# Attention with a routed feed-forward: row sums out of the bank ring, normalisations on ScalarE, expert order, one power on GpSimd

## What is computed

```python
router_probs = softmax(flat @ router_w + router_b)          # 8 experts
topk_probs, topk_idx = top_k(router_probs, 2)               # the other weights are 0
shared_out = gelu(flat @ sw1 + sb1) @ sw2 + sb2
h1 = gelu(einsum('td,edh->teh', flat, rw1) + rb1)           # hidden 256
mixed = einsum('ted,te->td', einsum('teh,ehd->ted', h1, rw2) + rb2, weights)
out = shared_out + mixed
```

## Time and profile before

| | |
|---|---|
| runs | 468.04, 468.20, 470.07 us; median 468.2 |
| the profiled execution | 470.0 us; its span, first to last instruction, 468.2 us |
| mean granted clock of TensorE | 0.984 of full speed |
| TensorE busy | 450.0 us (96%) |
| GpSimd, VectorE, ScalarE busy | 307.6, 276.1, 203.8 us |
| attention alone, then experts beside the end of attention | to about 395 us, then to 468 us |

### The profile page before, as it was taken

The page is one execution under the profiler, slowest core; times in us unless marked ns, Lnnn a source line. Parts: engine busy times, 40 slices in busy tenths (PEclk is TensorE's granted clock), DMA queues, the critical chain, the costliest instruction groups (busy, mean ns, idle before and its releaser), DMA issues.

```text
span 468.2 us, 7198 instructions
## 1 busy us (share of the span) xinstructions
PE 450.0 (96%) x2567; PEld 336.3 (72%) x2567; DVE 276.1 (59%) x517; ACT 203.8 (44%) x293; POOL 307.6 (66%) x203
## 2 busy tenths in 40 slices
PE   9999899999999999999999999999999999997995
PEld 7777566877676777776777777767776676775884
DVE  4687965957644669665246687642464157743443
ACT  3553231323354334333642343335334465784772
POOL 5959583667366586774665867654559894765773
PEclk9999897999999999999999999999999999998999
DMA  8300200000002000000030000000000000000000
GB/s 241 92 1 1 53 2 0 2 1 0 2 0 54 1 0 1 0 1 2 0 97 6 1 0 2 1 0 1 1 1 2 0 1 0 1 0 1 24 3 22
DMA packets 5194, 7.27 MB, mean 16 GB/s; under 512 B 644, under 2 KB 4136, under 8 KB 5160
## 3 DMA queue, kind: packets, MB, share of 16 engines
q1 hardware_dynamic: 5160, 6.81, 5.2%
HBM read 6.29 MB, written 0.52 MB: 15 GB/s over the span
## 4 chain that ended last, share of the span: by engine, by line
PE 82%; POOL 6%; DVE 5%; issue 5%; ACT 1%; POOLq 0%; ACTq 0%; DVEq 0%
PE ps L1094 20%; PE ps L1000 11%; PE ps L1077 10%; PE ps L1078 10%; PE ps L1079 10%; POOL g_lo L633 5%; PE ps L924 5%; PE ps L926 4%; PE ps L925 4%; PE ps L1012 2%; DVE ps L829 2%; PE ps L1018 1%; PE ps L1006 1%; PE ps L932 1%; DVE xn L771 1%
## 5 line engine op out<-in xcount | busy, mean ns | idle before, releaser
L697 ACT ACTIVATE probs<-ps 128x1024 f32<-128x1024 f32 (+1 forms) x112 | 107.8, 963 | 160.0 <-PE ps L1079 158.8
L486 POOL TENSOR_TENSOR work<-work,probs 128x1024 f32<-128x1024 f32 x60 | 142.7, 2378 | 44.9 <-ACT probs L697 42.7
L816 DVE TENSOR_REDUCE maxes<-ps 128x1 f32<-128x402 f32 x256 | 134.2, 568 | 31.9 <-PE ps L1000 31.3
L1094 PE MATMUL ps<-probs,v_sb 128*64 128x256 f32 (+1 forms) x832 | 98.1, 386 | 0.0
L1077 PE MATMUL ps<-g_hi,ctxT_hi 97*128 97x512 f32 (+1 forms) x208 | 84.2, 405 | 1.1 <-DVE g_hi L824 1.1
L1094 PEld LDWEIGHTS ps<-probs,v_sb 128*64 128x64 f32 (+1 forms) x832 | 57.4, 138 | 36.7 <-issue 9.8
L1000 PE MATMUL ps<-ctxT_hi,g_hi 96*128 96x402 f32 x256 | 79.8, 374 | 4.0 <-DVE maxes L816 2.0
L1078 PE MATMUL ps<-g_lo,ctxT_hi 96*128 96x512 f32 (+1 forms) x208 | 82.8, 398 | 0.0
L1079 PE MATMUL ps<-g_hi,ctxT_lo 96*128 96x512 f32 (+1 forms) x208 | 82.4, 396 | 0.0
L1000 PEld LDWEIGHTS ps<-ctxT_hi,g_hi 96*128 96x128 f32 x256 | 47.2, 191 | 23.9 <-issue 6.4
L829 DVE RECIPROCAL ps<-ps 128x256 f32<-128x256 f32 x16 | 28.3, 1766 | 57.3 <-PE ps L1012 57.3
(11 more groups left out here) (138 smaller groups left out, 572.8 us busy)
## 6 DMA issues: line engine op xcount, KB each, us to landing
raw<-in_ctx_T_dram SPq DMA_DIRECT2D x3, 600.4 KB, 4.4
work<-in_L_ffn_rw_dram SPq DMA_DIRECT2D x1, 1024.0 KB, 7.6
raw<-in_ctx_T_dram SPq DMA_DIRECT2D x3, 150.8 KB, 2.6
x_sb<-in_x_dram SPq DMA_DIRECT2D x1, 384.0 KB, 5.2
early<-in_WqkT_dram SPq DMA_DIRECT2D x1, 336.0 KB, 4.7
wo_sb<-in_L_xattn_Wo_dram SPq DMA_DIRECT2D x1, 256.0 KB, 5.6
out_dram<-x_sb SPq DMA_DIRECT2D x1, 256.0 KB, 2.2
out_dram<-x_sb SPq DMA_DIRECT2D x2, 128.0 KB, 1.7
```

Source lines behind the costliest of these rows:

```text
L486: ops.tensor_tensor(acc, acc, pr, ALU.add).then_inc(summed, 1)
L697: nc.scalar.activation(probs[0:rows, n % SLOTS, 0:wide, :], s, ACT.Exp, scale=SCALE).then_inc(probs_ready, 1)
L816: v.tensor_reduce(maxes[:, p % 2, i * T + t, blk:blk + 1], src[:, 0:BW], AX.X, ALU.max).then_inc(ring_taken, 1)
L1094: ins = mm(o_bank[DH * i:DH * (i + 1), :], v_sb[0:rows, c, h * DH:(h + 1) * DH], probs[0:rows, n % SLOTS, j, i * S:(i + 1) * S], start=(c ...
```

## The change

The row sums leave the ring for the first 14 pairs: they go into the bank that the one-chunk unit of the next pair leaves free, with semaphores of their own, and the score tile that next uses that bank waits until they are taken. The second layernorm step (`normal`, `norm`) is done by ScalarE as `rstd * x + shift`, except for the first batch's first one; GpSimd makes `shift`. The planner no longer counts `normal` and `norm` among VectorE's costs. `g` of the second pair is placed ahead of the last two `v0`. In the second half the shared expert comes last, and `wrow` goes before the first `spread`. VectorE makes the low parts of the last four items. The largest logit is subtracted on VectorE, so that the exponentials are one instruction; in the second half they are a power of e on GpSimd, and `best` is done by VectorE.

```diff
-DVE_US = {"max": 0.51, "g": 1.45, "shift": 0.72, "sums": 2.3, "y": 0.5, "yt": 1.8, "norm": 1.6, "xt": 0.95,
-          "xn": 1.5, "router": 0.5, "rank": 2.6, "wrow": 0.7, "stats": 1.3, "normal": 1.6}
+DVE_US = {"max": 0.51, "g": 1.45, "shift": 0.72, "sums": 2.3, "y": 0.5, "yt": 1.8, "xt": 0.95,
+          "xn": 1.5, "router": 0.5, "rank": 2.6, "wrow": 0.7, "stats": 1.3}
...
-            tasks += rest[:2] + [("shift", b, p)] + rest[2:] + [("g",) + order[1]]
+            tasks += rest[:2] + [("shift", b, p)] + rest[2:-2] + [("g",) + order[1]] + rest[-2:]
...
-                        main.append(("ring", ("sums", qb, qp)))
+                        main.append(("ring", ("sums", qb, qp)) if (b, p) == order[-1] else ("sums", (qb, qp)))
...
+        if name == "sums" and x[0] != "ring":
+            pe += PE_US[name]
+            dve = max(dve, pe + HOP_US) + DVE_US[name]
+            return
...
+def expert_order(half, experts):
+
+    return [experts] + list(range(experts)) if half == 0 else list(range(experts)) + [experts]
...
+            if h == 1 and turn == 0:
+                out.append(("ring", ("wrow", last)))
             if e < experts:
                 out.append(("ring", ("spread", h, e)))
...
-            if h == 1 and turn == 0:
-                out.append(("ring", ("wrow", last)))
...
+        def sums_bank(pair):
+
+            return s_bank((pair + 2) * NU - 1, 1)[:, 0:S]
...
+        LAST_SUMS = B * PAIRS - 2
+
+        def sums_done(pair):
+
+            w = ("sums",) + divmod(pair, PAIRS)
+            return (sums_taken, pair + 1) if pair < LAST_SUMS else taken(w)
...
-        LAST_LO = NI - HK
+        LAST_LO = NI - 2 * HK
...
-                    engine.wait_ge(ring_filled, ring_no[("sums",) + divmod(pair - 2, PAIRS)] + 1)
+                    engine.wait_ge(sums_filled, pair - 1)
...
             def inverse_roots(tiles, round_no):
                 pool.wait_ge(var_ready, round_no)
...
+                then_own(g.tensor_tensor(rstd[:, tiles], veps[:, tiles], neg_half[:, tiles], ALU.pow))
+                g.tensor_tensor(shift[:, tiles], neg_mean[:, tiles], rstd[:, tiles], ALU.mult).then_inc(rstd_ready, 1)
...
+            g.memset(euler[:], math.e)
...
+                if kind == "exp" and w == NHALF - 1:
+                    pool.wait_ge(logit_ready, w + 1)
+                    g.tensor_tensor(lexp[:], euler[:], logit[:], ALU.pow).then_inc(lexp_ready, 1)
+                if kind == "best" and w < NHALF - 1:
...
+            def normal(src, tiles, round_no):
+
+                act.wait_ge(rstd_ready, round_no)
+                for t in tiles:
+                    ins = nc.scalar.activation(xn[:, t, :], src[:, t, :], ACT.Identity, bias=shift[:, t:t + 1],
+                                               scale=rstd[:, t:t + 1])
+                ins.then_inc(xn_ready, 1)
...
+                elif kind == "normal":
+                    normal(x_sb, range(w * T, w * T + T), w + 1)
+                elif kind == "norm":
+                    if w == 0:
+                        act.wait_ge(*taken(("xn", 1)))
+                    normal(x1, range(w * T, (w + 1) * T), B + w + 1)
...
-                elif kind == "exp":
+                elif kind == "exp" and w < NHALF - 1:
                     act.wait_ge(logit_ready, w + 1)
-                    for t in range(TH):
-                        ins = nc.scalar.activation(lexp[:, t, :], logit[:, t, :], ACT.Exp,
-                                                   bias=neg_lmax[:, t:t + 1])
-                    ins.then_inc(lexp_ready, 1)
+                    nc.scalar.activation(lexp[:], logit[:], ACT.Exp).then_inc(lexp_ready, 1)
...
+                v.tensor_scalar(neg_mean[:, ts], mv[:, ts, 0], -1.0, None, ALU.mult)
...
+            def quotient(b, p, rden, signal):
+
+                pair = b * PAIRS + p
+                v.reciprocal(rden, rden).then_inc(rden_ready, 1)
+                dve.wait_ge(rden_ready, pair + 1)
+                dve.wait_ge(o_raw_ready, pair + 1)
+                v.tensor_tensor(oT[:, b % 2, p, :], o_raw[:], rden, ALU.mult).then_inc(signal, 1)
...
+                if kind == "sums":
+                    dve.wait_ge(sums_filled, w[0] * PAIRS + w[1] + 1)
+                    quotient(*w, sums_bank(w[0] * PAIRS + w[1]), sums_taken)
...
-                        v.tensor_reduce(neg_lmax[:], logit[:], AX.X, ALU.max, negate=True).then_inc(logit_ready, 1)
+                        then_own(v.tensor_reduce(neg_lmax[:], logit[:], AX.X, ALU.max, negate=True))
+                        v.tensor_tensor(logit[:], logit[:], neg_lmax[:].unsqueeze(2).to_broadcast([P, TH, E]), ALU.add
+                                        ).then_inc(logit_ready, 1)
...
-                elif kind == "norm":
-                    normal(x1, range(w * T, (w + 1) * T), B + w + 1)
...
+                elif kind == "best" and w == NHALF - 1:
+                    dve.wait_ge(ranked, w + 1)
+                    dve.wait_ge(wrow_zero, 2)
+                    then_own(v.tensor_tensor(weight[:], rprob[:, :, 0:E], low[:, :, 0:E], ALU.subtract))
+                    then_own(v.tensor_copy(w_hi[:], weight[:]))
+                    hi = w_hi[:].bitcast(F32)
+                    wr = wrow[:, w * TH:(w + 1) * TH, :]
+                    v.tensor_copy(wr[:, :, 0:E], hi)
+                    v.tensor_tensor(wr[:, :, WLO:WLO + E], weight[:], hi, ALU.subtract).then_inc(w_ready, 1)
...
+                if kind == "sums":
+                    pair = w[0] * PAIRS + w[1]
+
+                    pe.wait_ge(probs_ready, (pair + 2) * NU - 2)
+                    row_sums(*w, sums_bank(pair)).then_inc(sums_filled, 1)
...
+                    if u == 1 and j == 1 and n > 2 * NU:
+
+                        pe.wait_ge(sums_taken, min(b * PAIRS + p - 1, LAST_SUMS))
```

More of the change, by code:

```diff
@@ L16 @@
+import math
 from contextlib import ExitStack
@@ L211, in plan_experts @@
     for h in range(halves):
-        for turn, e in enumerate([experts] + list(range(experts))):
+        for turn, e in enumerate(expert_order(h, experts)):
             new = list(range(n, n + chunks))
             out += [("first", i) for i in new]
+            if h == 1 and turn == 0:
+                out.append(("ring", ("wrow", last)))
             if e < experts:
@@ L298, in build @@
         rstd = sb("rstd", [P, NT])
+        shift = sb("shift", [P, NT])
+        neg_mean = sb("neg_mean", [P, NT])
         neg_half = sb("neg_half", [P, NT])
@@ L349, in build @@
         lexp = sb("lexp", [P, TH, E])
+        euler = sb("euler", [P, TH, E])
         lsum = sb("lsum", [P, TH])
@@ L455, in build @@
         block = ctx.enter_context(nc.Block())
-        items = [(h, e, k) for h in range(NHALF) for e in [E] + list(range(E)) for k in range(HK)]
+        items = [(h, e, k) for h in range(NHALF) for e in expert_order(h, E) for k in range(HK)]
         NI = len(items)
-        LAST_LO = NI - HK
+        LAST_LO = NI - 2 * HK
         weighed, count = {}, 0
@@ L702, in _ @@
                     if pair:
-                        act.wait_ge(*taken(("sums",) + divmod(pair - 1, PAIRS)))
+                        act.wait_ge(*sums_done(pair - 1))
                     nc.scalar.copy(o_raw[:], o_bank).then_inc(o_raw_ready, 1)
-                elif kind == "exp":
+                elif kind == "exp" and w < NHALF - 1:
                     act.wait_ge(logit_ready, w + 1)
-                    for t in range(TH):
-                        ins = nc.scalar.activation(lexp[:, t, :], logit[:, t, :], ACT.Exp,
-                                                   bias=neg_lmax[:, t:t + 1])
-                    ins.then_inc(lexp_ready, 1)
+                    nc.scalar.activation(lexp[:], logit[:], ACT.Exp).then_inc(lexp_ready, 1)
                 elif kind == "split":
@@ L765, in moments @@
                 ts = slice(tiles[0], tiles[-1] + 1)
+                v.tensor_scalar(neg_mean[:, ts], mv[:, ts, 0], -1.0, None, ALU.mult)
                 v.tensor_scalar(veps[:, ts], mv[:, ts, 1], LN_EPS, None, ALU.add).then_inc(var_ready, 1)
-            def normal(src, tiles, round_no):
-                dve.wait_ge(rstd_ready, round_no)
-                for t in tiles:
-                    ins = v.tensor_scalar(xn[:, t, :], src[:, t, :], mv[:, t, 0:1], rstd[:, t:t + 1],
-                                          ALU.subtract, ALU.mult)
-                ins.then_inc(xn_ready, 1)
+            def quotient(b, p, rden, signal):
[4 more added lines that the diff above has]
+                v.tensor_tensor(oT[:, b % 2, p, :], o_raw[:], rden, ALU.mult).then_inc(signal, 1)
             dve.wait_ge(s_x0, 16)
             moments(x_sb, range(T))
-            normal(x_sb, range(T), 1)
+            dve.wait_ge(rstd_ready, 1)
+            for t in range(T):
+                ins = v.tensor_scalar(xn[:, t, :], x_sb[:, t, :], mv[:, t, 0:1], rstd[:, t:t + 1],
+                                      ALU.subtract, ALU.mult)
+            ins.then_inc(xn0_ready, 1)
             dve.wait_ge(first_ready, 1)
@@ L826, in _ @@
```

(28 more changed lines are left out.)

14 lines of the change are left out of this document (8 added, 6 removed).

## The result

| | before | changed |
|---|---|---|
| runs | 20, 467.88 to 472.67 us | 20, 463.92 to 468.31 us |
| median | 470.09 us | 467.33 us |
| the profiled execution | 470.0 us (span 468.2) | 465.87 us (span 464.1) |
| granted clock | 0.984 | 0.985 |

The ratio is 0.994, 95% interval 0.992 to 0.996: 2.8 us faster, and 467.33 lies outside the range of 448 to 461. The kernel is faster, as forecast, but by under a quarter of the 12.4 us. A small part is the base: the three runs that the forecast was set against have a median of 468.2, twenty have 470.09. Against the one base 11.5 us are missing, against the other 9.6.

The account below looks back on a forecast made before the run. TensorE, 96% busy, bounds the kernel; only its idle spells and half-clock stretches can give time. Terms 0.9 + 3.7 + 3.2 + 4.9 - 1.4 + 1.1 = 12.4 us take the 468.2 median to 455.8; range 448 to 461.

Parts of the forecast that it names:

- Part 1: At 25 us, `g` of the second pair ahead of the last two `v0` shortens the maxima's wait: gain 0.9 us.
- Part 2: Normalisations move from VectorE to ScalarE, removing a 1.97 us TensorE idle spell and half a slow stretch: gain 3.7 us.
- The stall at 70 us: TensorE's waits for a maximum and the shift row, with the half-clock work after them, go: gain 4.9 us.
- Part 3: Row sums leave the three-bank ring, so three value projections of next batches no longer wait for the quotient: gain 3.2 us.
- Rival six: No change: shortened waits reappear at the next releaser, GpSimd's adds; about 468 us, chance 0.04.
- rival five: Slower: planner's new order puts maxima and shift right behind quotients, stalls of 4.9 us each; three give 470.5; chance 0.05.
- Part 4's "nothing" for the first half: First half's router exponentials in one instruction, after VectorE's subtraction, lie under attention: no gain or cost.
- Parts 4 and 5: Expert turns around the half change: 4.9 to be had, less power's wait 3.7, clock 1.7, spread's wait 0.9: -1.4 us.
- Part 6: Tail: VectorE makes the last four low parts in place of GpSimd, ending near 461.0 instead of 462.2: gain 1.1 us.
- The fourth rival: Ranking and `best` on VectorE wait for GpSimd's splits at the shared port: 453 to 454 with a cheap power; chance 0.05.
- first (cheap): GpSimd's 32-column power takes only 0.77 to 2 us and TensorE keeps its clock: 450.4 to 451.6 us, chance 0.24.
- second (dear) power: GpSimd's 32-column power takes 8.2 us, leaving TensorE 7.4 us idle: 459.5 us in all, chance 0.20.

Follow-up runs that it names:

- e10: e9 with the row sums in the spare bank and at most one maximum before a new batch's first value projection: 451.44 us.
- e4: The changed kernel with the row sums of all pairs back in the ring, no spare bank and no guard: 463.43 us.
- e8: e4 with all router exponentials on ScalarE and the maximum subtracted as a bias in both halves: 456.27 us.
- e5: The changed kernel with the seven later normalisations back on VectorE, the planner's costs left as changed: 482.67 us.
- e2: The changed kernel with the first half's router maximum subtracted by ScalarE as a bias again, not by VectorE: 464.28 us.
- e1: The changed kernel with the second half's router exponentials on ScalarE again, ranking and `best` staying on VectorE: 463.03 us.
- e9: e8 with the spread and weighing of the second half's first turn placed behind the second products: 454.53 us.
- e11: e9 with `best` of the second half on GpSimd, as in the kernel before: 457.89 us.
- e6: The changed kernel with lone powers of 1 to 64 columns added at the end of GpSimd's queue: 486.81 us, one run.

## Why the prediction was wrong

**Its reading of the profile** held: what counts is TensorE's idle spells and the slow stretches, and the differences between these kernels are read from them. e10, with no wait over 1 us and the clock at 1.0, is the fastest. The leads below are those of the two profiled executions, whose spans differ by 4.1 us where the medians differ by 2.8.

**Part 1** (0.9): pair 0 starts 2.1 us earlier, but the start of the span itself shifts between executions (24.90 to 26.07 in kernels with the same beginning, e4 and e8 to e10). Right in sign; the size can't be told to better than about 1 us.

**Part 2** (3.7) held in its mechanism. A tile takes 0.48 us on ScalarE against my 0.45, and the idle spell at 50 us is gone with its slow stretch.

**The stall at 70 us** (4.9) was gained, but not for the reason I gave. I had put it to Part 3 and to VectorE coming late from `normal`. e4 has no spare bank and e5 has the normalisations on VectorE, and neither has the stall. What they share is the order: without the costs of `normal` and `norm` the planner puts the shift row ahead of the quotient. I had named the planner in half a sentence and priced nothing by it, so this term came out right by luck. It and Part 2 together are 8.6 us; from pair 0 to pair 3 the lead grew by 10.2 - 2.1 = 8.1.

**Part 3, the three v waits** (3.2), is the first step that failed. "Those banks are emptied by ScalarE, which is free": true of the banks that other projections hold, not here, where the three items ahead of the projection are maxima, queued on VectorE behind the quotient. I had looked for who held the bank and not for who stands in the three places ahead once it is gone. It cost 3.9 us instead (e4, with what is said there of the clock), a miss of 7.1. Rival six (the wait reappears at the next releaser) named the mechanism, but with GpSimd as the releaser; rival five put several maxima behind the quotient and took the stall to be paid at a shift row.

**Part 4's "nothing" for the first half** is the second. The subtraction does not "lie under attention": the maxima that TensorE needs stand behind it in VectorE's queue. 0.19 us became 1.82, and the whole cost 3.1 (e2).

**Parts 4 and 5** (-1.4) is the third. The two turns that I had at 11.41 us in the kernel before, with 6.5 needed, took 425.19 - 411.77 = 13.42: 2.0 us lost where I had 4.9 - 3.7 - 1.7 = -0.5. Three terms were mis-sized. The turns need more than 6.5: kernels without the power and without `best` on GpSimd take 7.31 to 7.77 us for them (e1, e9, e10), so 3.6 to 4.1 us were to be had and not 4.9. The power costs 0.159 us a column and not 0.125, so 5.43 us in place of 4.45, and the idle spell was 4.48 in place of 3.7. The slow stretch was 6.82 us, not 3.41, though e2 and e4 show 3.41 behind the same idle spell. The turn after them lost 1.0 us, for which I had 0.9. So -3.0 in all, 1.6 worse than I had it. e1 shows that the step itself should not have been made: `best` on VectorE alone is worth 3.4 us (e11), and the power takes 4.3. The spread's wait was 0.87 against my 0.9, and e9 removes it.

**Part 6** (1.1) held: the lead grew by 4.1 - 2.6 = 1.5 us to the end. One spread of 0.23 us of it is only moved, from the last turn to the first of that half, since the shared expert has none.

The three failed steps are 7.1 + 3.1 + 1.6 = 11.8 us. The sum of 12.4 less these leaves 0.6 us, where the medians differ by 2.8. Of the 2.2 between them, 0.7 are in the lead by pair 3 (10.2 against 0.9 + 3.7 + 4.9 = 9.5) and 0.4 in the tail; the other 1.1 I can't assign, and it is less than the interval of e2 or e4 alone. The range was too narrow because it gave each term bounds of its own cost, but let none of the "nothing" terms become a loss.

**The fourth rival** (the shared port at `best`) is in the rows: L932 and L933 take 1.19 and 1.20 us beside GpSimd's splits. It costs nothing there, since TensorE was late by then from the power. The first (cheap) and second (dear) power are both out, by e6.

What stays open: why a slow stretch follows some idle spells and not others of the same length. No run varied the length of the spell alone.

## What to carry to other kernels

When a buffer is taken out of a ring, ask which items then stand in the places ahead of the next taker, and on which engine's queue they are read: the wait goes only if they are read earlier than the one removed. Before an operation is costed at nothing, look at what stands behind it in its engine's queue and what the other engines do at that moment; an instruction of 0.19 us can last as long as the neighbour's big one. And a change of a kernel with a planner is two changes, the one to the engines and the one to the order: the stall at 70 us went by the order alone, and the spare bank that cost 3.9 us with three maxima ahead of the projection stands in a kernel 3.1 us faster than e9 with one.

## What the hardware showed beyond that

A power on GpSimd costs 0.159 us a column, 75 times a simple operation's 2.13 ns, for both pairs of operands tried; all exponentials together took ScalarE 0.23 us and two table loads of 1.28.

In the changed kernel idle spells of TensorE of 1.36 and 1.50 us were followed by a slow stretch at 205 and 273 us, and spells of 1.36 by none at 111 and 305. Shorter ones can be followed by one too: 1.17 us in e1 (425.21) and e8 (418.09), and in the kernel before 1.05 at 70.42, with the stretch from 71.27. The value projections' waits of 1.04 to 1.08 us in the kernel before, e4, e8, e9 and e11 were followed by none.

What one slow stretch of 3.41 us costs can be estimated from runs of one kernel at different clocks, since each takes some 0.0037 off the mean. The changed kernel's runs have 463.9 us at 0.989, about 465.9 at 0.985 and about 467.4 at 0.982: 1.5 to 2.0 us a stretch. The kernel before, beside e1 to e4, went from 468.0 us at 0.992 to 472.7 at 0.977: 1.2 us a stretch. With the clock at 0.999 to 1.0 the six runs of e10 lie within 0.52 us.
